# Sixty-four routed experts on one core: single tiles for the last eight, a rotation of three accumulators, and a tail in which VectorE does every addition

## The reference, cut to what matters

```
x  = x + tanh(g_xattn) * xattn(layernorm(x), ctx)
h  = layernorm(x)                            # 2048 tokens of 256
w, i = top 6 of 64 experts, out of the 3 best of 8 groups
slot = i * 96 + min(position of the token in expert i, 95)
buf[slot] = h[token]                         # the last writer wins slot 95
out[e] = (silu(buf[e] @ Wg[e].T) * (buf[e] @ Wu[e].T)) @ Wd[e].T     # 64 experts, 96 slots
y  = sum over the 6 choices of w * out[slot]
x  = x + tanh(g_ffn) * (y + silu(h @ Sg.T) * (h @ Su.T) @ Sd.T)
```

## Time and profile before

| | us |
|---|---|
| median of 3 runs | 362.18 |
| lowest and highest | 361.76, 364.5 |
| the profiled execution, whole program | 362.74 |
| its span, first to last instruction | 361.0 |
| what lies around the span (362.74 - 361.0) | 1.74 |
| mean granted TensorE clock | 0.985 |

### The profile page before, as it was taken

One profiled execution on the slowest core, in us unless ns is written; L12 is line 12 of the kernel. 1 busy time (PEld: TensorE's weight loads), 2 busy tenths in 40 slices (PEclk: granted clock), 3 DMA queues, 4 the chain that ended last, 5 costly groups with the idle time before them and its releaser, 6 DMA issues.

```text
span 361.0 us, 7995 instructions
## 1 busy us (share of the span) xinstructions
PE 321.7 (89%) x2317; PEld 274.1 (76%) x2317; DVE 245.5 (68%) x910; ACT 156.2 (43%) x448; POOL 161.4 (45%) x176
## 2 busy tenths in 40 slices
PE   1787989898999999989999999999998999999833
PEld 0566778787787978878888888888787888978711
DVE  5832868777877778785566666666655667758676
ACT  2467676668667772511334343333333333321000
POOL 7902020202020220306478778877887777555000
PEclk9999999999999999998999999999999999999978
DMA  7993283769756162442499999999999758776995
GB/s 264 363 291 92 64 243 91 236 235 302 261 187 256 36 277 105 182 127 78 117 264 308 318 320 310 319 307 309 284 290 302 149 90 209 159 159 159 330 412 203
DMA packets 34274, 81.31 MB, mean 225 GB/s; under 512 B 6832, under 2 KB 15552, under 8 KB 34240
## 3 DMA queue, kind: packets, MB, share of 16 engines
q1 hardware_dynamic: 22000, 61.38, 51.2%
q0 software_dynamic: 9216, 14.16, 19.5%
q10 hardware_dynamic: 3024, 5.35, 4.6%
HBM read 58.49 MB, written 22.32 MB: 224 GB/s over the span
## 4 chain that ended last, share of the span: by engine, by line
PE 56%; DMA 21%; issue 7%; ACT 6%; DVE 5%; POOL 3%; ACTq 1%; SPq 0%; DVEq 0%; POOLq 0%
PE bank L400 50%; DMA acc_rows<-th_sb,sidx 6%; DMA qk_sb<-xn_rows,gidx 4%; DMA d_ring<-acc_rows 3%; DMA w_ring<-acc_rows 3%; DMA acc_rows<-pt_sb,sidx 3%; ACT p_sb L849 3%; PE bank L436 2%; POOL acc_rows L1786 2%; PE bank L638 2%; ACT xn L817 1%; DMA acc_rows<-act_t,sidx 1%; POOL p_sb L1772 1%; PE bank L461 1%; DMA x_all<-x_in 1%
## 5 line engine op out<-in xcount | busy, mean ns | idle before, releaser
L400 PE MATMUL bank<-hi_hot,w_ring 128*112 128x96 f32 (+1 forms) x768 | 88.4, 265 | 0.6 <-ACT hi_hot L995 0.6
L400 PEld LDWEIGHTS bank<-hi_hot,w_ring 128*112 128x112 f32 (+1 forms) x768 | 85.7, 182 | 2.5 <-issue 0.8
L400 PE MATMUL bank<-d_ring,xn 112*96 112x256 f32 (+1 forms) x256 | 66.1, 380 | 0.6 <-DVE xn L1523 0.6
L1001 ACT ACTIVATE h_sb<-bank 128x192 f32<-128x192 f32 x64 | 21.2, 331 | 61.4 <-PE bank L400 61.4
L1521 DVE TENSOR_TENSOR xn<-h_sb,bank 112x96 f32<-112x96 f32 x64 | 16.3, 254 | 41.2 <-ACT h_sb L1001 40.9
L400 PEld LDWEIGHTS bank<-d_ring,xn 112*96 112x96 f32 (+1 forms) x256 | 36.9, 163 | 7.8 <-DVE xn L1523 0.8
L1751 POOL TENSOR_TENSOR guess<-var,nhalf 128x2 f32<-128x2 f32 (+1 forms) x8 | 7.7, 958 | 73.8 <-DVE var L1350 73.8
L1786 POOL DMA_INDIRECT acc_rows<-pt_sb,sidx x18 | 29.1, 1616 | 13.1 <-ACT pt_sb L1011 4.4
L995 ACT ACTIVATE hi_hot<-bank 128x256 f32<-128x256 f32 x48 | 18.5, 384 | 36.2 <-PE bank L638 25.4
L1743 POOL TENSOR_SCALAR zeros<-zeros,token 128x256 f16<-128x256 f16 x14 | 12.8, 930 | 38.0 <-DVE zeros L1302 38.0
L1786 POOL DMA_INDIRECT acc_rows<-th_sb,sidx x15 | 23.7, 1581 | 8.8 <-issue 3.1
(11 more groups left out here) (212 smaller groups left out, 657.8 us busy)
## 6 DMA issues: line engine op xcount, KB each, us to landing
w_ring<-wgu_in SPq DMA_DIRECT2D x32, 704.0 KB
acc_rows<-w_ring SPq DMA_DIRECT2D x5, 2176.0 KB, 7.7
d_ring<-wd_in SPq DMA_DIRECT2D x32, 224.0 KB
d_ring<-wd_in SPq DMA_DIRECT2D x32, 128.0 KB
d_ring<-acc_rows SPq DMA_DIRECT2D x8, 512.0 KB, 4.2
w_ring<-acc_rows SPq DMA_DIRECT2D x8, 512.0 KB, 7.1
xn_rows<-xn SPq DMA_DIRECT2D x8, 256.0 KB, 3.3
w_ring<-acc_rows ACTq DMA_DIRECT2D x4, 512.0 KB, 10.3
```

What stands on the lines that cost most here:

```text
L400: return pe.matmul(o, lhsT, rhs, start=start, stop=stop, skip_group_check=True)
L1001: act.activation(silu_sb[:, e % 2, :], eg_ps[e % 2][:, 0:2 * C], ACT.Silu).then_inc(s["silu_ready"], 1)
```

## The change

Experts 56 to 63 are no longer packed. Each gets a tile of its own with 96 rows, so that there are 50 tiles: 0 to 41 as before, 42 to 49 for experts 56 to 63. Their targets go round 0, 1, 2. `add_up` waits for the tile two before it for tiles 36 to 43 and for the tile three before it for all others; the waits for the tile just before are gone. `column` finds a tile's place in the tables: the eight experts' tables are made by the old ones and two more columns (`NAMED + q`). A fourth output buffer (`p_sb`) holds tiles 48 and 49. Eight gathers and eight additions have 96 rows and two of each are new.

The buffers of the read-backs are permuted, so that target 3 waits for expert 47 and not 55. Its last two quarters are issued one after the other. Target 2 is read when tile 47 has landed, 0 when 48 has and 1 when 49 has, all by SyncE. The result is written in eight pieces, by SyncE and ScalarE in turn.

The splitting into bf16 parts is gone. `w_over_t` and `last_sb` are zeroed in their lower halves once and the 16 products are fp32, half of them (`SUMS[0:4]`: pairs 0, 1, 2, 5) before the last shared group's second and third part, the others at the end. TensorE adds no target any more; VectorE adds all five and all sums, in a new order.

```diff
-THREE = 14
-PE_ADDS = (4, 5, 6, 7)
+SPLIT_BLKS = 14
+SPLIT = SPLIT_BLKS * EB
+SPLIT_TILES = SPLIT_BLKS * EB_TILES
+TILES = SPLIT_TILES + E - SPLIT
+LATE_ROT = 3
+SUMS = (0, 1, 2, 5, 3, 4, 6, 7)
+EARLY_SUMS = 4
+ADD_FIRST = E - 10
...
+        def next_tile(e):
+            if e >= SPLIT:
+                t = tile_of(e) + EB_TILES
+                return t if t < TILES else None
+            return tile_of(e) + EB_TILES if e % EB else None
+        def slots_of(t):
+            return P if t < SPLIT_TILES else C
+        def column(t):
+            if t < SPLIT_TILES:
+                return t
+            q, j = divmod(t - SPLIT_TILES, EB)
+            return SPLIT_TILES + EB_TILES * q + j - 1 if j else NAMED + q
...
             def add_up(t):
                 pool.wait_ge(s["o_ready"], t + 1)
-                pool.wait_ge(s["d_ready"], t + 1)
-                if EB_TILES <= t <= FOUR * EB_TILES:
-                    pool.wait_ge(s[f"acc_in{(t - EB_TILES) % ADDS}"], 16 * ((t - EB_TILES) // ADDS + 1))
-                if t >= FOUR * EB_TILES:
-                    pool.wait_ge(s[f"acc_in{(t - 2) % ADDS}"], 16 * ((t - 2) // ADDS + 1))
-                if t >= THREE * EB_TILES and t % EB_TILES == 0:
-                    pool.wait_ge(s[f"acc_in{(t - 1) % ADDS}"], 16 * ((t - 1) // ADDS + 1))
+                if t < SPLIT_TILES:
+                    pool.wait_ge(s["d_ready"], t + 1)
+                flight = 2 if FOUR * EB_TILES <= t < SPLIT_TILES + 2 else 3
+                if t >= EB_TILES:
+                    pool.wait_ge(s[f"acc_in{(t - flight) % ADDS}"], 16 * ((t - flight) // ADDS + 1))
...
-            for k, t, e in ((4, FOUR * EB_TILES - 1, FOUR * EB), (3, (FOUR + 1) * EB_TILES - 1, THREE * EB)):
+            for k, t in ((4, FOUR * EB_TILES - 1), (3, (FOUR + 1) * EB_TILES - 1)):
                 wait_added(sp, t)
-                sp.wait_ge(s["o_done"], e)
+                sp.wait_ge(s["o_done"], FOUR * EB)
                 for q in range(QUARTERS):
                     read_back(sp, k, q)
-                    sp.wait_ge(s[f"back{k}_{q}"], 16)
-            for k, t in ((0, TILES - 2), (2, TILES - 1)):
+                    if k == 4 or q < 2:
+                        sp.wait_ge(s[f"back{k}_{q}"], 16)
+            for k, t in ((2, TILES - 3), (0, TILES - 2), (1, TILES - 1)):
                 wait_added(sp, t)
                 for q in range(QUARTERS):
                     read_back(sp, k, q)
...
             for e in range(1, E):
-                if e % EB and e // EB + 1 < BLKS:
-                    turn_rows(tile_of(e) + EB_TILES)
+                if next_tile(e) is not None:
+                    turn_rows(next_tile(e))
                 up(e)
...
+            def add_lasts(pairs):
+                for r in pairs:
+                    for i in range(2):
+                        t = 2 * r + i
+                        last = mm(sum_ps[r][:, i * L:(i + 1) * L], w_over_t[:, t * P:(t + 1) * P], last_sb,
+                                  start=i == 0 and r not in (2 * (Q_TAIL - NQ) + 1, PAIRS - 1), stop=i == 1)
+                    last.then_inc(s["ov_done"], 1)
+            late_up(Q_TAIL + 1, 0)
+            tail_down(Q_TAIL)
...
+            add_lasts(SUMS[0:EARLY_SUMS])
+            late_up(Q_TAIL + 1, 1)
+            late_up(Q_TAIL + 1, 2)
+            tail_down(Q_TAIL + 1)
+            add_lasts(SUMS[EARLY_SUMS:PAIRS])
...
+            def add_to(r, operand, sem, value, to="added"):
+                dve.wait_ge(s[sem], value)
+                wait(dve, s["added"], added[r])
+                if to == "added":
+                    added[r] = add_to.n = add_to.n + 1
+                dve.tensor_tensor(pair(x_all, r), pair(x_all, r), operand, ALU.add).then_inc(s[to], 1)
...
             tail_act(Q_TAIL, 0)
-            add_back(3, 0)
-            add_back(3, 1)
+            add_back(3, 2)
             tail_act(Q_TAIL, 1)
-            add_back(3, 2)
+            add_back(3, 3)
             tail_act(Q_TAIL, 2)
-            add_back(3, 3)
             add_back(3, 4)
+            add_back(3, 5)
+            add_back(2, 0)
+            add_back(2, 1)
             tail_act(Q_TAIL + 1, 0)
             add_back(3, 6)
             add_back(3, 7)
+            add_back(2, 2)
+            add_back(2, 3)
+            for r in SUMS[0:EARLY_SUMS]:
+                add_sum(r)
+            add_back(2, 4)
+            add_back(2, 5)
+            tail_act(Q_TAIL + 1, 1)
+            add_back(2, 6)
+            add_back(2, 7)
             tail_act(Q_TAIL + 1, 2)
-            for r in range(ADDED_BY_POOL, PAIRS):
-                add_back(0, r, "added3")
+            for r in range(PAIRS):
+                add_back(0, r)
+            for r in range(PAIRS):
+                if r in SUMS[EARLY_SUMS:]:
+                    add_sum(r)
+                add_back(1, r, "sum_ready")
```

More of the change, by code:

```diff
@@ L72 @@
 OUT_BLKS = 3
+LASTS_IN = (32 * 5 + 16, 32 * 5, 32 * 4 + 16, 16)
 ADDS = 4
@@ L757, in _ @@
+            late_up(Q_TAIL + 1, 0)
+            tail_down(Q_TAIL)
+            for k, n in enumerate(LASTS_IN):
+                pe.wait_ge(s[f"lasts_in{k}"], n)
+            pe.wait_ge(s["w_pad_ready"], 1)
+            pe.wait_ge(s["last_pad_ready"], 1)
             pe.wait_ge(s["o_ready"], TILES)
             pe.wait_ge(s["at_out"], E)
-            pe.wait_ge(s["act_ready"], 3 * PAIRS)
-            for r in range(PAIRS):
-                for i in range(2):
-                    t = 2 * r + i
-                    pe.wait_ge(s["w_parts_ready"], t + 1)
-                    for k, part in enumerate((high_mid[:, t * P:(t + 1) * P], high_mid[:, t * P:(t + 1) * P], high_low[t])):
-                        last = mm(sum_ps[r][:, i * L:(i + 1) * L], part, last_parts[:, k, :],
-                           start=i == 0 and k == 0 and r not in (2 * (Q_TAIL - NQ) + 1, PAIRS - 1), stop=False)
-                if r not in PE_ADDS:
-                    last.then_inc(s["ov_done"], 1)
@@ L1056, in _ @@
                         tail_silu(q, m)
-            wait_added(act, TILES - 1)
-            for q in range(QUARTERS):
-                read_back(act, 1, q)
+            for r in range(1, PAIRS, 2):
+                write_out(act, r)
         @block.vector
@@ new lines, in add_to, with add_back @@
+            def add_to(r, operand, sem, value, to="added"):
[4 more added lines that the diff above has]
+                dve.tensor_tensor(pair(x_all, r), pair(x_all, r), operand, ALU.add).then_inc(s[to], 1)
+            add_to.n = 0
+            def add_back(k, r, to="added"):
+                add_to(r, pair(back[k], r), f"back{k}_{r * QUARTERS // PAIRS}", 16, to)
@@ L1582, in _, with add_sum @@
+            def add_sum(r, to="added"):
+                add_to(r, sum_ps[r][:, :], "ov_done", SUMS.index(r) + 1, to)
+            dve.memset(last_sb[E:P, :], 0.0).then_inc(s["last_pad_ready"], 1)
             dve.wait_ge(s["xn_saved"], 16 * PAIRS)
@@ L1625, in _ @@
             tail_act(Q_TAIL, 1)
-            add_back(3, 2)
+            add_back(3, 3)
             tail_act(Q_TAIL, 2)
-            add_back(3, 3)
             add_back(3, 4)
-            high, middle, low_high = [last_parts[:, k, :] for k in range(3)]
-            go = Steps(dve, s["last_part_step"], 0)
-            for k in range(OUT_BLKS):
-                dve.wait_ge(s[f"lasts_in{k}"], 32 * len(range(k, BLKS, OUT_BLKS)))
-            go.did(dve.tensor_copy(last_sb[E:P, :], last_sb[0:E, :]))
```

283 lines of the change are left out of this document (132 added, 151 removed).

## The result

| | before | after |
|---|---|---|
| median of 20 runs each, us | 363.63 (361.53 to 367.14) | 361.67 (359.35 to 365.39) |
| ratio, 95% interval | 1 | 0.9946 [0.9922, 0.997] |
| profiled execution, whole program, us | 362.74 | 362.08 |
| its span, us | 361.0 | 360.3 |
| mean granted TensorE clock | 0.985 | 0.975 |

The change is worth 2.0 us. The forecast was 2.7 (359.5 against 362.18), and its range held the time. In a later set of runs the changed kernel stood at 0.9943 [0.9909, 0.9977], so the gain is small and real. That the two profiled spans differ by only 0.7 us is the scatter of single executions, which is some 1% here.

A forecast was written before the change was run, and what follows sets the result against it. Bound: serial waits between indirect additions, then the last read-back. Target 2's first quarter at 332.9, VectorE's 22.6 us row to 355.5, plus 2.9 gives span 358.4; plus 1.74 is 360.1, median 0.56 lower: 359.5, range 356.0 to 364.0.

The forecast's parts named there:

- What sets the end: Tail: serial waits between indirect additions delay the reads before the change; afterwards VectorE's row behind target 2's first quarter ends last.
- VectorE's count: Tail: 34 additions and sums and three tail_act from target 2's first quarter on, 22.6 us, ending at 355.5.
- the smaller last write: End of span: last write of 256 KB instead of 512, half of 0.6 us saved, 2.9 us after the last addition.
- The loop up to tile 41: Expert loop: unchanged in time up to tile 41, with tile 41 issued at 313.29.
- I take the first: GpSimd's gathers: cost follows the rows, so eight smaller ones save 2.0 us and two new ones cost 2.1.
- the other bound: GpSimd's gathers: if their cost is fixed whatever the rows, GpSimd is 2.6 us later at tile 41.
- The pace of the additions: Late tiles on GpSimd: 1.2 us per addition of 96 rows plus 0.3 between, with some waits for landings.
- The reads: Read-backs of targets 2, 0 and 1: 6.3 MB at 418 GB/s, 15.1 us, over at 346, hidden behind VectorE.
- Rival 1: Chain of additions runs faster: tile 47 issued at 322.4, landed 326.2, total 357.0, range 356 to 358; chance 0.24.
- Rival 2: TensorE's clock falls to a half in its idle gap before the late products and stays down: 361.4; chance 0.12.
- Rival 3: Three additions in flight slow each other: at 9.45 us per landing, tile 47 lands 339.1, 369.9 in all; chance 0.12.
- Rival 4: Fixed-cost gathers and TensorE's waits push tiles 40 and 41 back 3 us; tile 47 no earlier, 362.5; chance 0.10.

The follow-up runs named there:

- e2: The changed kernel, but add_up waits for the tile two before, not three before, for tiles 44 to 49 as well; 1.0015 of the kernel before.
- after again: A second profiled execution of the changed kernel, nothing altered; VectorE's row ran from 334.09 to 356.59 us.
- e4: The kernel before with the 16 products of the last rows in fp32 and all splitting into bf16 parts removed; 0.9984 of the kernel before.
- e6: The kernel before with VectorE adding all eight pairs of target 2 and TensorE none; 1.0075 of the kernel before.
- e13: The kernel before, plus GpSimd zeroing all of w_over_t in the set-up and ScalarE waiting for it; 1.0021 of the kernel before.
- e5: The changed kernel with VectorE's non-waiting additions and sums moved ahead of add_back(2, 0), and TensorE adding pairs 3 and 7 of target 2; 0.9868 of the kernel before.
- e12: Repeat in a later set: the changed kernel with VectorE reordered, TensorE adding two pairs of target 2, and no zeroing; 0.9882 of the kernel before.
- e9: The changed kernel with VectorE reordered, TensorE adding two pairs of target 2, and no zeroing, first run; 0.9831 of the kernel before.

## Where the prediction was right and where it failed, point by point

**What sets the end: right.** The chain, `e2` and the unbroken row of VectorE show it. One reading of the trace before was wrong: its last 45 us do go through engines at their end, TensorE's identity products for target 2 and then VectorE's last sums.

```profile
349.75 4.75 PE bank L400 x6
```

VectorE's count held: 22.6 us worked out, 22.5 measured here, in `e2` and in after again (334.09 to 356.59). What lies behind it was 2.5 us (357.83 to 360.3), not 2.9: the smaller last write gives more than the half that I took.

**The terms of the sum, by the profiled execution.** Tile 47 landed at 331.62 and not at 328.6: 3.0 late. Its issue makes 2.7 of that (327.13 for 324.4). The quarter landed 3.7 us after tile 47 and not 4.3 (-0.6), the row was 0.1 shorter, the end 0.4 shorter. 358.4 + 3.0 - 0.6 - 0.1 - 0.4 = 360.3, the span.

**The step that failed: "The loop up to tile 41. I take this as unchanged."** Tile 40 left at 311.66 instead of 308.91. Before tile 42, 2.5 us are lost (317.98 for 315.5), and after it almost nothing: 9.15 us from 42 to 47 where I had 8.9. The step rested on "I take the first, since GpSimd has less to name with fewer rows", and the rows after show a cost nearly fixed: 0.06 us saved per gather where I had 0.25, so that two gathers more are a loss of about 2 us on GpSimd and no wash. I had this as the other bound, "GpSimd is 2.6 us later at tile 41", and took the wrong end. Tile 42 still waited for a landing, that of tile 40, for 2.01 us. The other profiles bear the step's failure out: from the issue of tile 38 to that of tile 40, with the two new gathers between, it is 6.2 to 6.4 us in all ten profiles with single tiles and 4.6 to 4.9 in the four with packed ones (before, `e4`, `e6`, `e13`). So what I had put at nothing costs 1.3 to 1.8 us at tile 40.

Not all of that loss reached tile 47. In after the loop began 1.6 us later than in the profile of before, which leaves 1.1 of tile 47's 2.7 for GpSimd. In after again it began 0.8 us later and tile 47 was issued at 325.93, 1.5 late, which leaves 0.7. The later beginning is in no step of mine beyond the 0.2 us for four naming products. In after the stretch at the half clock, 1.7 us, is as much as all of it; why the loop of after again began 0.8 us later, without that stretch, stayed open.

**The pace of the additions: right by two errors.** I had 1.5 us between them (1.2 + 0.3) and got 1.73, but I had also let tile 43 wait for tile 41's landing, 2.4 us behind 42, where it came after 1.76.

**The reads: hidden, as forecast, but not because they were "over at 346".** The last quarter of target 1 landed at 351.0: tile 49, in front of that target, took 8.6 us to land, and from 334 to 338 us the queues moved 335 GB/s at a busy share of 0.99, not 418. The narrower places are earlier. Target 2's second quarter landed at 337.75 and was taken up at 338.18. Target 0's first quarter landed at 342.10, and VectorE took it up at 344.97. That margin was 2.9 us, and `e5` and `e12` are what happens when it is used up.

**Rival 1 (a faster chain)** did not come: the smaller gathers gave nothing. **Rival 2 (the clock)** came in its harmless form. The clock was at a half from 342.1 to 349.0 and returned after about 4 us of products, as the trace of before had it. The first late sum was ready at 350.73 and wanted at 351.59, so 0.9 us of the "3 us" to spare remained. The rule of the Trainium skill, "TensorE: Matmul & The Clock Gate", section "HAM oscillation — how this bites in real kernels", that the group of matmuls behind such a gap starts cold, agrees with the 4.76 us against 2.76; that it costs time is what this tail avoids. **Rival 3 (additions slow each other)** is right about beside-the-reads landings (8.6 us) and wrong about the place: tiles 44 and 47, which it had in series, landed in 3.7 and 4.5, and tile 43, for which tile 46 really waited, in 4.9, all under its 5.5. **Rival 4 (no gain at all)** named the step that failed: gathers of fixed cost, and a tile 40 that is 2.7 us late. Its first quarter at 335.9 is nearer to the 335.35 of after than my 332.9, and the span that belongs to it (358.4 + 3.0 = 361.4) is nearer to the 360.3 than my 358.4. What it had wrong is that tile 47 is then as late as before: it was issued 4.8 us ahead of the last tile before (327.13 against 331.91). The fp32 products and the shorter VectorE list are worth nothing that can be told, as forecast (`e4`).

**The number itself.** 361.67 is 2.2 over 359.5. Of that, 1.45 is no error of the working: the kernel before had a median of 363.63 over 20 runs, where the three shown gave 362.18. The other 0.7 is the working's own error, from median to median. That it is so small is in part luck: for the profiled execution the working gave 358.4 and 360.3 was measured, so that this pair of profiles shows a gain of 0.7 us where 2.6 was worked out, and the scatter of single executions covers the difference. I had also written that one per cent is "about what can be told from no change here". 20 runs each tell a quarter of that, and the result, half a per cent, is inside my "same" and outside the interval of no change: calling it "same" rested on a noise that was put four times too high.

## What to carry to other kernels

When the tail is a fixed row of instructions behind one landing, count that row from the durations in the profile and put the work into when its first input lands; the count was right to 0.1 us, the landing was off by 3. Splitting an indirect transfer into smaller ones is no wash where its issuing engine is near its limit: take its cost as fixed until a row shows otherwise. And a difference at the front of the trace that one profile of each kernel shows is worth nothing until the same kernel has been profiled twice.

## What was not expected of the hardware

- An indirect DMA's cost on GpSimd hardly depends on its rows: 0.99 to 0.93 us for a gather, 1.57 to 1.43 for an addition, at 128 and 96 rows.
- An indirect addition that is issued between 1.1 us ahead of target 2's 512 KB reads and 2.8 us behind their start lands after 5.7 to 9.9 us, where one issued 1.7 us or more ahead took 3.3 to 3.7. GpSimd's instruction itself lasted 3.0 to 3.5 us instead of 1.43 in three of these (`e5`, `e9`, `e12`).
- TensorE's clock can fall to a half at a fixed place (about 141 us) in one execution of a kernel and not in the next, for 1.7 us of the path. Four products near 17 us take 2.05 us in some executions and 1.10 in others, with 1.6 us lost in all. What decides either stayed open.
